# Attention's output projection as three products of rounded halves

## What is computed

```python
q = (x @ W_q).reshape(Bq, T1_, N_HEAD, D_HEAD).transpose(0, 2, 1, 3)
k = (context @ W_k).reshape(Bq, T2_, N_HEAD, D_HEAD).transpose(0, 2, 1, 3)
v = (context @ W_v).reshape(Bq, T2_, N_HEAD, D_HEAD).transpose(0, 2, 1, 3)
scores = jnp.einsum('bhqd,bhkd->bhqk', q, k) * atten_scale
scores = scores + bias[None, None, :, :] * head_scale[None, :, None, None]
attn = jax.nn.softmax(scores, axis=-1)
out = jnp.einsum('bhqk,bhkd->bqhd', attn, v).reshape(Bq, T1_, N_HEAD * D_HEAD)
return out @ W_out + b_out
```

## Time and profile before

| | us |
|---|---|
| median of 3 runs (2122.62 to 2124.55) | 2124.15 |
| the profiled execution | 2128.7 |
| its span, first to last instruction | 2127.0 |
| TensorE busy | 1853.9 (87%) |
| VectorE busy | 1312.3 (62%) |
| ScalarE busy | 997.5 (47%) |
| GpSimd busy | 593.7 (28%) |
| L1114, 1024 records of TensorE | 235.6 |

### The profile page before, as it was taken

One profiled execution on the slowest core, in us unless ns is written; L12 is line 12 of the kernel. 1 busy time (PEld: TensorE's weight loads), 2 busy tenths in 40 slices (PEclk: granted clock), 3 DMA queues, 4 the chain that ended last, 5 costly groups with the idle time before them and its releaser, 6 DMA issues. The chain is left out here.

```text
span 2127.0 us, 43848 instructions
## 1 busy us (share of the span) xinstructions
PE 1853.9 (87%) x14851; PEld 1671.5 (79%) x14851; DVE 1312.3 (62%) x3630; ACT 997.5 (47%) x2467; POOL 593.7 (28%) x712
## 2 busy tenths in 40 slices
PE   5999999999996599958999999999994699999920
PEld 4888888888885488847888888888883699999920
DVE  2677877877877233336778777878874444444423
ACT  3776677676674133334554454454551333333300
POOL 0012222222232200024243433434312422222056
PEclk9999999999998799978999999999997799999965
DMA  5676011011000599941111111111100422232134
GB/s 196 244 273 241 27 37 37 25 37 36 25 28 24 183 298 298 295 163 46 36 46 46 51 36 44 48 46 43 43 16 30 149 88 88 84 111 67 35 105 147
DMA packets 121821, 205.95 MB, mean 97 GB/s; under 512 B 15856, under 2 KB 63505, under 8 KB 121680
## 3 DMA queue, kind: packets, MB, share of 16 engines
q1 hardware_dynamic: 99408, 145.14, 20.1%
q0 software_dynamic: 22272, 59.05, 8.9%
HBM read 111.56 MB, written 94.37 MB: 97 GB/s over the span
## 5 line engine op out<-in xcount | busy, mean ns | idle before, releaser
L469 POOL DMA_INDIRECT buf<-a_rxn,a_disp x192 | 197.3, 1028 | 253.6 <-DVE comb L853 90.2
L1114 PE MATMUL a_psM<-a_wo,a_oT 128*128 128x256 f32 x1024 | 235.6, 383 | 4.5 <-ACT a_oT L621 1.4
L600 ACT ACTIVATE a_S<-a_S,a_mn 128x128 f32<-128x128 f32 x512 | 199.0, 396 | 68.8 <-DVE a_mn L889 68.8
L1114 PEld LDWEIGHTS a_psM<-a_wo,a_oT 128*128 128x128 f32 x1024 | 192.6, 191 | 36.0 <-issue 3.4
L79 PE MATMUL e_psH<-e_x_hi,e_w_hi 128*128 128x256 f32 x640 | 184.9, 289 | 0.0
L869 DVE TENSOR_TENSOR a_S<-a_S,a_rz 128x512 f32<-128x512 f32 x256 | 177.5, 693 | 8.8
L81 PE MATMUL e_psH<-e_x_hi,e_w_lo 128*128 128x256 f32 x640 | 181.7, 284 | 0.0
L80 PE MATMUL e_psH<-e_x_lo,e_w_hi 128*128 128x256 f32 x640 | 181.6, 284 | 0.0
L79 PE MATMUL a_psP<-a_c_hi,a_wk_hi 128*128 128x256 f32 x512 | 155.4, 303 | 11.1 <-DVE a_c_lo L746 11.1
L79 PE MATMUL a_psP<-a_x_hi,a_wq_hi 128*128 128x256 f32 x512 | 157.5, 308 | 5.2 <-DVE a_x_lo L746 5.2
L1077 PE MATMUL a_psT<-ident,a_S 128*128 128x128 f32 x1024 | 139.3, 275 | 18.7 <-DVE a_S L869 18.7
(11 more groups left out here) (184 smaller groups left out, 4904.6 us busy)
## 6 DMA issues: line engine op xcount, KB each, us to landing
y<-e_y SPq DMA_DIRECT2D x104, 256.0 KB, 2.9
buf<-a_zeros SPq DMA_DIRECT2D x16, 1280.0 KB, 7.0
buf<-a_zeros SPq DMA_DIRECT2D x16, 1024.0 KB, 5.9
e_rows<-buf SPq DMA_DIRECT2D x64, 256.0 KB, 3.9
e_w_in<-in_L_ffn_w SPq DMA_DIRECT2D x64, 256.0 KB, 3.2
a_ctx<-in_ctx SPq DMA_DIRECT2D x32, 256.0 KB, 2.9
e_w_out<-in_L_ffn_w SPq DMA_DIRECT2D x64, 128.0 KB, 3.8
e_w<-in_L_ffn_W_in SPq DMA_DIRECT2D x8, 1024.0 KB, 6.8
```

The costliest lines, as they stand in the source:

```text
L469: g_.indirect_dma_start(out=buf, out_offset=bass.IndirectOffsetOnAxis(ap=disp[:, par, i, k:k + 1], axis=0), in_=rxn[:, par, i], in_offset= ...
L600: ins = a.activation(s[:, h], s[:, h], ACT.Exp, bias=mn[:, u % 2, h:h + 1], scale=-1.0, accum_out=z[:, u % 2, h:h + 1])
L1114: ins = mm(psM[:, 0], oT[:, c], wo[:, c], start=c == 0, stop=c == HP - 1)
```

## The change

W_out is loaded into the upper half of `qT` (`raw_wo`), behind the load of x and behind a wait for the split of W_v, and is split once per layer: ScalarE writes `wo_hi` at the end of its prologue, VectorE writes `wo_lo` in its own. Every step, ScalarE's evacuation of psV writes `o_hi` in place of `oT`, and VectorE has a new instruction, `heads_lo`, between `read_scores(g, 2 * w + 1)` and `invert(g, 2 * w + 1)`: it subtracts `o_hi` from psV into `o_lo`. TensorE's two waits for ScalarE's evacuation of the heads (in `weigh_values` and in `project_out`) are now waits for VectorE's instruction (`s_ol`). `project_out` issues 24 products of halves in place of 8 float32 ones. ScalarE's first write into the upper half of qT for queries of group 1 waits until the split of W_out is done. Layer 0's semaphores are held until the end of the experts' phase and cleared there by one GpSimd instruction; the renaming of `m.sem` to `sem` that this needs is left out of the diff.

```diff
+        wo_hi = m.sb(L + "wo_hi", [P, HP, D], F32R)
+        wo_lo = m.sb(L + "wo_lo", [P, HP, D], F32R)
...
+        raw_wo = qT[:, 1].rearrange("p h n -> p (h n)").rearrange("p (c n) -> p c n", c=HP)
...
-        oT = m.sb(L + "oT", [P, HP, P])
+        o_hi = m.sb(L + "o_hi", [P, HP, P], F32R)
+        o_lo = m.sb(L + "o_lo", [P, HP, P], F32R)
...
-            sp.dma_start(wo[:], d["L0_xattn_W_out" if first else "L1_xattn_Wo"].rearrange("(c p) n -> p c n", p=P)
-                         ).then_inc(s_late, 16)
             if first:
                 sp.dma_start(t.x[:, 2 * GT:NB], d["x"][2 * GT:NB].rearrange("b p d -> p b d")).then_inc(t.s_rest, 16)
+            sp.wait_ge(s_w["v"], 18)
+            sp.dma_start(raw_wo, d["L0_xattn_W_out" if first else "L1_xattn_Wo"].rearrange("(c p) n -> p c n", p=P)
+                         ).then_inc(s_wol, 16)
...
+                if g == 1 and j == 8:
+                    act.wait_ge(s_wos, 2)
...
-                    a.activation(oT[:, half * 4:half * 4 + 4], psV[:], ACT.Copy).then_inc(s_oT, 1)
+                    a.activation(o_hi[:, half * 4:half * 4 + 4], psV[:], ACT.Copy).then_inc(s_oT, 1)
...
                 for j in range(8, NJ):
                     evac_job(0, 0, j)
+                act.wait_ge(s_wol, 16)
+                a.activation(wo_hi[:], raw_wo, ACT.Copy).then_inc(s_wos, 1)
...
+            def heads_lo(g, w):
+                u = 2 * w
+                if has(g, u, 4):
+                    half = (w - 2) % 2
+                    ve.wait_ge(s_oT, at(g, UG // 2, w - 1))
+                    v_.tensor_tensor(o_lo[:, half * 4:half * 4 + 4], psV[:], o_hi[:, half * 4:half * 4 + 4].bitcast(F32),
+                                     ALU.subtract).then_inc(s_ol, 1)
+
+            def w_out_lo():
+                ve.wait_ge(s_wos, 1)
+                v_.tensor_tensor(wo_lo[:], raw_wo, wo_hi[:].bitcast(F32), ALU.subtract).then_inc(s_wos, 1)
...
                 read_scores(g, 2 * w + 1)
+                heads_lo(g, w)
                 invert(g, 2 * w + 1)
...
                     split_in(0, x_hi, x_lo, s_xT)
+                    w_out_lo()
                     ve.wait_ge(t.s_rest, 16 * 6)
...
                 inputs(1)
+                w_out_lo()
...
-                        pe.wait_ge(s_oT, at(g, UG // 2, u // 2 - 1))
+                        pe.wait_ge(s_ol, at(g, UG // 2, u // 2 - 1))
...
-                    pe.wait_ge(s_oT, at(g, UG // 2, 4 * i // 2 + 2))
+                    pe.wait_ge(s_ol, at(g, UG // 2, 4 * i // 2 + 2))
...
-                        pe.wait_ge(s_late, 32)
+                        pe.wait_ge(s_late, 16)
+                        pe.wait_ge(s_wos, 2)
                     for c in range(HP):
-                        ins = mm(psM[:, 0], oT[:, c], wo[:, c], start=c == 0, stop=c == HP - 1)
+                        ins = split_product(nc.tensor, psM[:, 0], o_hi[:, c], o_lo[:, c], wo_hi[:, c], wo_lo[:, c],
+                                            c == 0, c == HP - 1)
...
+        @block.gpsimd
+        def _(pool):
+            nc.clear_and_free_semaphores(t.done_sems)
```

More of the change, by code:

```diff
@@ L97, in sem, with lasting_sem @@
         return self.stack.enter_context(self.nc.semaphore(name))
+    def lasting_sem(self, name):
+        return self.nc.alloc_semaphore(name=name)
 def row_vector(ap, n):
@@ new lines, in attention @@
+        s_tc = sem(L + "context_transposed")
+        NS = 3
+        s_xT = sem(L + "x_transposes_evacuated")
+        s_cT = sem(L + "context_transposes_evacuated")
+        s_pj = sem(L + "projected")
+        s_ev = [sem(L + f"projection_evacuated{i}") for i in range(2)]
+        s_sc = sem(L + "scores_ready")
+        s_read = sem(L + "scores_read")
+        s_exp = sem(L + "exp_ready")
+        RZ = 1 if first else 2
+        s_rz = sem(L + ("sums_inverted" if first else "sums_then_inverse_ready"))
```

101 lines of the change are left out of this document (50 added, 51 removed).

## The result

The changed kernel takes 2174.96 us (median of 4 runs, 2167.44 to 2178.19) against 2123.6 us (4 runs, 2122.62 to 2124.55): a ratio of 1.024, 95% interval 1.021 to 1.027. It is slower, as forecast, but by 51 us where 30 were forecast, and it lies 5 us above the range. The profiled execution took 2171.84 us, its span is 2170.1.

The account below looks back on a forecast made before the run. TensorE was taken to bound layer 0, around a two-step VectorE chain, and a closed VectorE chain three of layer 1's four steps. Layer 0's +9.2 and layer 1's +20.9 us made +30.1: 2154 us, range 2134 to 2170.

Parts of the forecast that it names:

- a group without the jump: Loop groups: +0.31 to +0.41 us each in layer 0, +1.53 in nine of layer 1's twelve.
- the signs that I had named: Changed profile: longer layer 1 groups, TensorE waiting for o_lo, lower TensorE share, step 1's wait 0.3 us shorter, layer 0 a third.
- the 45.1: Layer 1's loop: a group with the jump was to take 45.1 us where it took 43.24.
- The step that failed: the jump: Layer 1's three groups with the loop's jump: +1.83 us each, as ScalarE's chain had already given its 0.30.
- the ends: Last groups: layer 0 +3.3 us, between 0 and +4.4, with three more heads_lo in VectorE's chain; layer 1 +1.5.
- TensorE's gain: Output projection: 24 products in 2.88 us against eight float32 ones in 3.55, a gain of 0.67 us each.
- the even case: Rival: layer 0's subtractions find room (-16 us for its groups), layer 1 shares the cycle; 2122 us, chance 0.05.
- TensorE stays the bound: Rival: all heads_lo fit in VectorE's free fifth, all 64 gains on the path; 2081 us, chance 0.08.
- The rule of the passes: Projection: FP32 as four passes would make three products cost 3/4, 2.66 us, gain 0.89; the rows' 0.81 was used.
- The head of layer 0: Ahead of layer 0's first group: W_out's split delays the first reading, +2.65 us, between 0 and +3.5.
- The head of layer 1: Layer 1's prologue: VectorE's half partly beside a GpSimd round trip, +0.95 us, between 0 and +4.2.
- nothing is hidden: Rival: every heads_lo costs 0.61 us without TensorE's gain in return; 2186 us, chance 0.07.

Follow-up runs that it names:

- e8: The changed kernel with layer 1's sums of the exponentials made by ScalarE in place of VectorE: 2136.63 us, ratio 1.005.
- e2: The kernel before with heads_lo alone, its low part written and waited for but not used, the product left float32: 2181.64 us, ratio 1.027.
- e6: The changed kernel with groups 4 to 11 written out in place of the loop, on every engine but SyncE: 2150.67 us, ratio 1.012.
- e10: The kernel before with groups 4 to 11 written out in place of the loop: 2117.87 us, ratio 0.997.
- e9: The changed kernel with heads_lo ahead of both readings of scores from the steps of group 15 on only: 2163.61 us, ratio 1.017.
- e1: The changed kernel without heads_lo per step, the heads' low parts written once ahead of the first group: 2125.76 us, ratio 0.999.
- e4: The kernel before with ten one-column copies more on VectorE in a turn of layer 0's loop: 2127.69 us, ratio 1.0014.
- e7: The kernel before with layer 1's sums of the exponentials made by ScalarE in place of VectorE: 2105.6 us, ratio 0.991.
- e11: The kernel before with ScalarE's sums of the exponentials in layer 1 and groups 4 to 11 written out: 2105.5 us, ratio 0.991.
- e14: The kernel before with 24 one-column copies more on VectorE in a turn of layer 0's loop, none in the prologue: 2133.09 us (one run).
- e12: The changed kernel with ScalarE's sums of the exponentials in layer 1 and groups 4 to 11 written out: 2124.75 us, ratio 0.999.
- e15: The changed kernel with ScalarE's sums in layer 1, groups 4 to 11 written out, and heads_lo ahead of the readings from group 15's steps: 2120.53 us, ratio 0.998.
- e5: The kernel before with ten one-column VectorE copies more in a turn of layer 0's loop and fifteen in the prologue: 2135.03 us, ratio 1.0038.

## Why the prediction was right and wrong

**The bound.** Right: VectorE's chain, open in layer 0 and closed in layer 1. The forecast for a group without the jump was +0.31 to +0.41 in layer 0, and 0.3 was measured; in layer 1 +1.53, and 1.5 was measured (1.1 with the groups written out). e8 shows that this cost hangs on VectorE's load. Of the signs that I had named, TensorE's wait for o_lo, its falling share and the shorter wait ahead of step 1's inverting (0.88 us at 1294.04 in layer 1, 0.2 less) are there. Two are not. From first reading to first reading, as the 45.1 was meant, the group up to the reading behind the jump takes 44.7 us (1288.51 to 1333.19), but the next one takes 43.7 and not 42.5, since the slower products behind the jump fall into it; together they are 0.9 over. And layer 0 has 18 of the 43 us by its last update, more than a third.

**The step that failed: the jump.** I had seen the 2.61 us of "issue" in layer 1, had taken it as something that comes with that loop, and priced the change at 1.83 in those groups. I never asked why layer 0's loop had none, and what the change would do to it. It had none by a few instructions. The subtractions in the loop and in the groups written out ahead of it move the loop's end from 811 to 835, and between 826 and 834 the stall begins. That is 3 x 1.5 us in layer 0 on the profiled execution (41.7 for 40.0, less the 0.2 us that the loop of before had). In layer 1 the stall was there before, and what is new is TensorE's lower clock behind it: 3 x 1.1 more than before (45.87 - 42.54 against 43.27 - 41.08), near the 1.2 that e2 gives. The prediction had no term for the clock. By the spans of the profiled executions the loop is 9.5 us of the change's cost, by the medians of e6 and e10 18 of the 51. The rest lies in how the profiled executions of before and after lie to their medians (8 us). A part of it can be TensorE's stall behind the jump in layer 1's experts, 5 to 6 us where it comes: the profiled execution of the changed kernel (2171.84) is without it, and its two slowest runs lie 6.3 higher. That is an estimate, as those runs have no trace.

**The term that was mis-sized: the ends.** +3.3 and +1.5 were forecast (+3.6 with group 14), +8.3 and +3.8 came. I had counted how long heads_lo takes in the last groups, and not what it stands behind. There TensorE has little else to do, its scores come late, VectorE waits for them in order, and TensorE waits for the instruction behind that wait. e9 shows that the place costs. With the waits comes the lower clock, which the term lacked as well: in layer 0's last two groups 17 us in place of 7 at a granted clock of 0.5. The upper bound of 4.4 for this term held no new wait and was no bound.

**TensorE's gain.** 0.56 a projection and not 0.67. More than that, both gains of a group were thought to be on the path: the -16 for layer 0's groups, were the subtraction off it, which the even case used, is refuted by e1, which gives -6.4. The rival "TensorE stays the bound" at 2081 was never open, though its time was worked out as if all 64 gains could be had.

**The rule of the passes.** The Trainium skill (FP8 and Floating Point Precision, TensorE Precision Notes) gives true FP32 four passes. My estimate from that, three passes for the products of halves and so 2.66 us, does not come out: the projection takes 2.96 to 3.07, 0.85 of the float32 form's 3.54 to 3.65. Whether float32 takes four passes no run here shows. The row's spacing was the better guide, and was still too low, for the gaps at the row's ends.

**The rest.** The head of layer 0 was about right. The first update of x comes 0.0 to 3.2 us earlier than in the profile of before in the kernels whose code up to it is the same (before, e4, e7, e10, e11, e14), on average 1.6 earlier, and from 0.8 earlier to 1.5 later in those with the changed head (after, e6, e8, e9, e12, e15), on average 0.6 later. The means lie 2.2 apart, where I had 2.65, with a spread of 2 to 3 in each. The head of layer 1 was too low by 2 in this execution. The 1.9 us between layer 0's last update and layer 1's start are not explained: e6, with the same split and clearing, has -1.0 there, so they need not be the change's. The range was too narrow since none of its bounds held a new wait or a lower clock; "nothing is hidden" at 2186 was the nearest rival by its number, and wrong in its mechanism.

## What to carry to other kernels

An engine's free time is worth something only at the place where the new instruction stands. Read what is queued ahead of it and whether that waits for the engine that will wait for it, at the ends of the pipeline as well as in the loop. If a trace shows an engine standing in "issue" behind a loop's jump, count each loop's instructions and where it ends before adding any to it, since the cost comes whole, and not by the instruction. And read the granted clock beside every new wait of TensorE: behind a wait of 2 to 3 us its products took nearly twice as long here for the next 3 to 7 us. And before making the costliest group of instructions cheaper, ask how much of its gain lies on the path: here the 0.56 us per projection was worth half in layer 0 and nearly nothing in layer 1, while moving the sums of one layer off the engine that binds there gained 20 us.

## What the runs showed of the hardware

- VectorE's jump back costs 0.3 us or 2.6 to 3.1 us. In layer 0 the dear one appears for a loop that ends between instructions 826 and 834 of its code or later: a loop of 339 instructions is without it (e4) and with it (e5), by where it ends; in layer 1 the loop from 1969 to 2330 is without it and the one from 2026 to 2396 has it. With it come 14 to 16 more packets on an instruction queue, for three jumps, and none passes there during a loop without it. What lies at these places in the code was not found.
- TensorE's loop of 656 instructions showed no such stall. Its loop of 806 instructions in layer 1's experts, at the same place in the code in five kernels, showed one of 2.3 to 2.4 us in three of five profiled executions, each with 9 more packets on the other instruction queue (85 and 76).
- Behind a wait of TensorE of 2.26 us for VectorE, at layer 1's jump, the granted clock was 0.50 for about 3.4 us, and products of 256 columns followed each other by 0.21 us in place of 0.12. Behind its wait of 1.26 us at the same place in the kernel before the clock stayed at 1.00.
- A product of rounded halves, 128 x 256, follows its forerunner by 0.12 us, but the last of a row leaves 0.09 us more and the first mostly 0.1 more, so 24 take 2.96 to 3.07 us against 3.54 to 3.65 for eight float32 products: 0.85.
- Four activations of 128x128 with accumulation on ScalarE replace one of 128x512 and a reduction on VectorE, and gain 0.9% of the whole, as they move 0.61 us per unit off the engine that binds.
- The changed kernel's four runs spread over 10.8 us, those of the same kernel without jumps over 3.3.
